# Layer 0 of a graph network: keys of two tiles of rows gathered with one weight load per block, and even and odd rounds of different order

## The chip, the cores and the metric

The kernel runs on one core of a Trainium2 chip. The metric is the device time of one execution in microseconds (us), as the median over several executions. The engines are TensorE (PE, with its weight loads as PEld), VectorE (DVE), ScalarE (ACT), GpSimd (POOL) and SyncE (SP); POOL and SP issue the DMAs.

## What is computed

There are 8192 nodes with 128 features, and an adjacency matrix of 8192 x 8192 int32 in which about one entry in 1024 is set (some 8 per row). Two graph attention layers follow one another; the change touches layer 0 alone.

```python
h = relu(layernorm(x))
e = (h @ Ws) @ (h @ Wt).T                      # Ws, Wt: 128 x 64
alpha = softmax(where(adj > 0, e, -9e15))      # over all 8192 nodes
x = x + alpha @ (h @ Wc)                       # layer 0
h = relu(layernorm(x))
# layer 1: another attention with leaky_relu scores, elu at the end, added to x
```

## The kernel before

**Tiles and selection.** The rows are worked on in 64 tiles of 128 rows. The nodes are held as 64 blocks (`NB`) of 128. For a tile the kernel doesn't score all 8192 nodes: from each block it picks up to 32 (`SLOT`) that some row of the tile has as a neighbour. For this DVE makes a 0/1 matrix `pick[:, b, block, slot]` (fp8, `make_pick`) out of the running count of marked nodes, which PE makes with one matmul against a triangle of ones (`prefix`) and DVE multiplies by the marks (`place`). A tile then has 64 x 32 = 2048 picked nodes.

**Gathering on PE.** The picks are matmul operands. `pick_keys(t, b, g)` has the keys `kp` of a block as weights (128 x 128) and 32 columns of `pick` as moving data, 16 blocks to a group, four groups g to a tile, and writes the PSUM bank `kg_ps`. `pick_values` and `pick_mask` have the pick as weights (32 columns of the array) and values or mask as moving data; each has four groups to a tile and one PSUM bank (`vg_ps`, `mg_ps`). ACT empties each bank after each group (`take_keys`, `take_values`, `take_mask`, 512 columns each), and the next group of the same kind waits for that: `wait(pe, k_evac, t * 4 + g)` and its likes.

**Scores and weighing.** `scores(t, b, q)` (q = 0 to 3) fills one of four PSUM banks from the gathered keys and mask; it waits for `k_evac` and `m_evac` of its group q and for the exponentials of the tile before. DVE takes the maximum of two banks at a time (`part_maximum`), spreads it (`spread_maximum`), PE transposes it (`turn_maximum`), DVE reduces it (`maximum`), ACT takes the exponentials of two banks at a time (`exps`), and PE weighs the values in four groups (`weigh`, 32 fp32 matmuls of 129 columns in all, of which the first group has one more). DVE divides and adds x (`denominator`, `finish`).

**Order.** Each engine runs the same sweep: round i works on tiles e = i-1, a = i-2, c = i-3 and d = i-4 at once, in an order written out by hand in `tile_step`. An engine does its instructions strictly in this order, waits included. Before, all rounds have one order; on PE it is: scores(c,3), values(c,2), mask(a,2), keys(a,1), values(c,3), mask(a,3), turn_maximum(c), keys(a,2), values(a,0), prefix(e), weigh(d,0 to 3), keys(a,3), scores(a,0), values(a,1), mask(e,0), scores(a,1), keys(e,0), mask(e,1), scores(a,2). Rounds 0 to 5 and 64 to 67 are written out, those between are a loop of two rounds. The first mask group of a tile waits for its `make_pick`.

**Adjacency.** POOL issues four DMAs per tile (`load_chunk`), each as soon as the mask group that read the same part of the buffer two tiles before is done.

Of the kernel before, what the change touches and what calls it, by code (L numbers as in the profile page):

```python
# [18 lines left out]
P = 128  # L19
# [28 lines left out]
def gnn_kernel(nc, x, xB, adj, adjB, Ws, Wt, Wc, W1, a1, out, x_mid, sel, sel_pick):  # L48
# [12 lines left out]
    with ExitStack() as ctx:  # L61
# [11 lines left out]
        def part(start, words, dt=F32):  # L73
# [5 lines left out]
            0, 8192, 16384, 20480, 28672, 32768, 34816, 36864, 40992, 43040, 44064, 45088, 46080)  # L79
# [14 lines left out]
        k_sel = part(K2, 1024, F16)  # L94
# [108 lines left out]
        kg_ps = ps[:, 4, :]  # L203
# [5 lines left out]
        mx_ps = ps[:, 7, 256:256 + P]  # L209
# [418 lines left out]
        def _(pe):  # L628
# [125 lines left out]
            def scores(t, b, q):  # L754

                pe.wait_ge(k_evac, t * 4 + (q + 1))
                pe.wait_ge(m_evac, t * 4 + (q + 1))
                wait(pe, p_done, t * 2 + (q // 2 - 1))
                settle()
                dst = s_ps[q]  # L760
                nc.tensor.matmul(dst, off_i, m_sel8[:, b, 4 * q:4 * q + 4, :].rearrange("p s n -> p (s n)"),  # L761
                                 start=True, stop=False, skip_group_check=True)
                for k in range(4):
                    at = (4 * q + k) * P
                    for n, rows in enumerate((cq_hi, cq_lo)):
                        last = nc.tensor.matmul(dst[:, k * P:(k + 1) * P], k_sel[:, at:at + P],  # L766
                                                rows[:, bass.ts(t, P)], start=False, stop=(n == 1),
                                                skip_group_check=True)
                last.then_inc(sc_done, 1)

            def turn_maximum(t):

                pe.wait_ge(mx_ready, t + 1)
                wait(pe, y_ready, t - 1)
                nc.tensor.transpose(mx_ps, mx_b[:, :], ident[:, :]).then_inc(mx_turned, 1)  # L775

            def weigh(t, b, g):

                pe.wait_ge(p_done, t * 2 + (g // 2 + 1))
                pe.wait_ge(v_evac, t * 4 + (g + 1))  # L780
                if g == 0:
                    wait(pe, y_ready, t)
                    pe.wait_ge(top_done, min(t + 2, TILES) if isinstance(t, int) else t + 2)
                    nc.tensor.matmul(pv_ps, ones_b[:, :], mean_rows[0], start=True, stop=False, skip_group_check=True)
                for k in range(4):
                    s = 4 * g + k
                    last = nc.tensor.matmul(pv_ps, p_T[:, s * P:(s + 1) * P], v_sel[:, b, s, :],  # L787
                                            start=False, stop=(s == SB - 1), skip_group_check=True)
                last.then_inc(pv_done, 1)

            def tile_step(i, b):
                e, a, c, d, cb = i - 1, i - 2, i - 3, i - 4, 1 - b
                if isinstance(i, int) and i == 2:
                    pe.wait_ge(mean_ready, 1)
                if isinstance(i, int) and i == 4:
                    pe.wait_ge(rows_ready, 1)
                if isinstance(i, int) and i == TILES + 2:
                    pe.wait_ge(m_evac, TILES * 4)
                    turn_weights(0, mg_ps)
                if isinstance(i, int) and i == TILES + 3:  # L800
                    score_vectors(0, mg_ps)
                if there(i, 3):
                    scores(c, cb, 3)
                    pick_values(c, cb, 2)
                if there(i, 2):
                    pick_mask(a, b, 2)
                    pick_keys(a, b, 1)
                if there(i, 3):
                    pick_values(c, cb, 3)
                if there(i, 2):  # L810
                    pick_mask(a, b, 3)
                if there(i, 3):
                    turn_maximum(c)
                if there(i, 2):
                    pick_keys(a, b, 2)
                    pick_values(a, b, 0)
                if within(i, EARLY + 1, TILES + 1):
                    prefix(e, pre_ps)
                if there(i, 4):
                    for g in range(4):  # L820
                        weigh(d, b, g)
                if there(i, 2):
                    pick_keys(a, b, 3)
                    scores(a, b, 0)
                    pick_values(a, b, 1)
                if there(i, 1):
                    pick_mask(e, cb, 0)
                if there(i, 2):
                    scores(a, b, 1)
                if there(i, 1):  # L830
                    pick_keys(e, cb, 0)
                    pick_mask(e, cb, 1)
                if there(i, 2):
                    scores(a, b, 2)
# [140 lines left out]
        def _(act):  # L975
# [132 lines left out]
            def take_keys(t, g):  # L1108

                act.wait_ge(kg_done, t * 4 + (g + 1))  # L1110
                nc.scalar.activation(k_sel[:, g * GW:(g + 1) * GW], kg_ps, ACT.Copy).then_inc(k_evac, 1)  # L1111
# [25 lines left out]
            def tile_step(i, b):  # L1137
                e, a, c, cb = i - 1, i - 2, i - 3, 1 - b
                if there(i, 3):
                    take_values(c, cb, 2)  # L1140
                if there(i, 2):
                    take_mask(a, b, 2)
                    take_keys(a, 1)
                if there(i, 3):
                    take_values(c, cb, 3)
                if there(i, 2):
                    take_mask(a, b, 3)
                    take_keys(a, 2)
                if there(i, 3):
                    exps(c, 0)  # L1150
                if there(i, 2):
                    take_values(a, b, 0)
                    take_keys(a, 3)
                if there(i, 3):
                    exps(c, 1)
                if there(i, 2):
                    take_values(a, b, 1)
                if there(i, 1):
                    take_mask(e, cb, 0)
                    take_keys(e, 0)  # L1160
                    take_mask(e, cb, 1)
# [140 lines left out]
        def _(dve):  # L1302
# [219 lines left out]
            def tile_step(i, b):  # L1522
# [3 lines left out]
                if there(i, 3):  # L1526
                    spread_maximum(c)
                if within(i, EARLY + 1, TILES + 1):
                    indicate(e, 1 - b, 1)
                if there(i, 3):  # L1530
# [17 lines left out]
                if there(i, 2):  # L1548
# [3 lines left out]
                if there(i, 2):  # L1552
                    part_maximum(a, 1)
# [421 lines left out]
```

## Time and the profile before

| | us |
|---|---|
| median of 3 runs | 1359.65 (1357.86 to 1359.94) |
| the profiled execution | 1364.51 |
| its span from first to last instruction | 1362.7 |
| around the span | 1.8 |
| mean granted TensorE clock | 0.979 |
| PE busy | 1270.7 (93%) |
| DVE busy | 1043.8 (77%) |
| ACT busy | 980.1 (72%) |

The first weighing of layer 0 starts at 108.6 us and the last at 903.5 us of the span; before it stands the preparation of the operands, behind it layer 1. Line 722 is the key matmul, 734 the values, 749 the mask, 761 and 766 the scores, 775 the transpose, 784 and 787 the weighing, 648 the prefix. ACT's lines are 1111 for keys, 1117 for values, 1126 for the mask and 1133 for the exponentials. DVE's are 1468 for `place`, 1477 for `make_pick` and 1486 for `part_maximum`.

In the timeline a row merges instructions of one kind that follow each other. Its duration for PE reaches to the end of the last matmul's results, while the next group starts earlier: the time that a group takes from PE is the distance to the start of the next row, where that did not wait.

### The profile page before, as it was taken

Reading aid. Unit: us, or ns where it says so; the run is one execution under the profiler, and the core shown is the slowest. Engines: PE = TensorE matmul, PEld = TensorE weight load, DVE = VectorE, ACT = ScalarE, POOL = GpSimd, SP = SyncE. Lnnn points to the kernel's source line nnn. Section 1 sums busy time; section 2 is a strip of 40 time slices with the busy share of each in tenths; the row PEclk is TensorE's granted clock in tenths of the full one; section 3 lists DMA queues with packets and bytes.
Section 4 is the critical chain, followed back from the end, with each engine's and each line's share of the span. In section 5 each row is a group of like instructions: output and inputs, shape, how many; then the busy total and the mean of one; then the engine's idle time right before and its main releaser. Section 6 shows DMA issues by size and latency. Waiting matters only on the chain.

```text
span 1362.7 us, 74732 instructions
## 1 busy us (share of the span) xinstructions
PE 1270.7 (93%) x31691; PEld 1125.0 (83%) x31691; DVE 1043.8 (77%) x2196; ACT 980.1 (72%) x2100; POOL 165.8 (12%) x331
## 2 busy tenths in 40 slices
PE   4868899999999999999999999988899999999996
PEld 3657788888888888888888888876899989999996
DVE  6846467767776766777777677657899989999997
ACT  4855466666666666666666666667898989999995
POOL 4210111111111111111111111012000000000000
PEclk9969899999999999999999999999899999999998
DMA  9773699999999999999999999610234334334332
GB/s 188 77 89 67 91 127 138 139 138 129 140 140 131 133 137 133 136 137 141 129 138 141 140 126 139 108 48 2 73 111 117 100 102 127 108 100 126 112 96 73
DMA packets 103503, 157.54 MB, mean 116 GB/s; under 512 B 11456, under 2 KB 36288, under 8 KB 102848
## 3 DMA queue, kind: packets, MB, share of 16 engines
q0 software_dynamic: 36864, 67.13, 52.4%
q1 hardware_dynamic: 66496, 88.37, 20.0%
q8 instruction: 107, 1.75, 0.5%
q14 instruction: 36, 0.29, 0.1%
HBM read 314.84 MB, written 41.94 MB: 262 GB/s over the span
## 4 chain that ended last, share of the span: by engine, by line
PE 76%; issue 9%; ACT 8%; DVE 4%; DMA 2%; POOL 1%; ACTq 0%; SPq 0%; DVEq 0%; POOLq 0%
PE ps L883 16%; PE ps L787 16%; PE ps L734 10%; PE ps L857 9%; PE ps L766 6%; PE ps L749 4%; PE ps L761 4%; PE ps L722 4%; ACT arena L1117 3%; ACT arena L1126 3%; PE ps L775 1%; DMA arena<-in_adjB 1%; PE ps L663 1%; PE ps L639 1%; PE ps L880 1%
## 5 line engine op out<-in xcount | busy, mean ns | idle before, releaser
L787 PE MATMUL ps<-arena 128*128 128x129 f32 x2048 | 246.6, 279 | 0.0
L883 PE MATMUL ps<-arena 128*128 128x129 f32 x2048 | 244.9, 278 | 0.7 <-issue 0.7
L1133 ACT ACTIVATE arena<-ps,neg_max 128x1024 f32<-128x1024 f32 x128 | 142.3, 1112 | 135.5 <-PE ps L787 135.5
L787 PEld LDWEIGHTS ps<-arena 128*128 128x128 f32 x2048 | 237.8, 194 | 0.0
L883 PEld LDWEIGHTS ps<-arena 128*128 128x128 f32 x2048 | 236.7, 194 | 0.9 <-issue 0.9
L1486 DVE TENSOR_REDUCE mx<-ps 128x1 f32<-128x1024 f32 x128 | 156.7, 1225 | 97.1 <-PE ps L766 92.7
L1117 ACT ACTIVATE arena<-ps 128x512 f32<-128x512 f32 x256 | 152.6, 596 | 100.9 <-PE ps L734 100.9
L589 POOL DMA_DIRECT2D arena<-in_adjB x256 | 136.6, 534 | 688.2 <-PE ps L749 672.6
L1691 DVE TENSOR_SCALAR arena<-arena 128x128 f32<-128x128 f32 x768 | 202.6, 341 | 15.0 <-issue 8.6
L1111 ACT ACTIVATE arena<-ps 128x512 f16<-128x512 f32 x256 | 153.6, 600 | 41.2 <-PE ps L722 38.6
L734 PE MATMUL ps<-arena 128*32 128x128 f16 x8192 | 164.7, 222 | 19.0 <-issue 9.3
L766 PEld LDWEIGHTS ps<-arena 128*128 128x128 f16 x2048 | 135.4, 98 | 31.0 <-issue 1.1
L1126 ACT ACTIVATE arena<-ps 128x512 fp8e4<-128x512 f32 x256 | 152.9, 597 | 10.9 <-PE ps L749 7.8
L857 PE MATMUL ps<-arena 128*32 128x132 f16 x8192 | 147.3, 226 | 14.2 <-ACT arena L1171 6.3
L1477 DVE TENSOR_TENSOR arena<-arena 128x2048 fp8e4<-128x2048 f16 x64 | 146.7, 2292 | 17.5 <-DVE arena L1468 17.3
L1171 ACT ACTIVATE arena<-ps 128x396 f32<-128x396 f32 (+1 forms) x384 | 144.6, 477 | 18.9 <-PE ps L857 18.9
L766 PE MATMUL ps<-arena 128*128 (+1 forms) x2048 | 157.7, 220 | 0.0
L1458 DVE TENSOR_REDUCE arena<-arena 128x32 f32<-128x1024 uint32 x128 | 154.9, 1210 | 1.6 <-DMA arena<-in_adjB 1.6
L734 PEld LDWEIGHTS ps<-arena 128*32 128x32 fp8e4 x8192 | 121.7, 97 | 40.1 <-issue 24.2
L857 PEld LDWEIGHTS ps<-arena 128*32 128x32 fp8e4 x8192 | 125.1, 98 | 32.4 <-ACT arena L1171 7.8
L1700 DVE SCALAR_TENSOR_TENSOR arena<-arena 128x1024 f32<-128x1024 fp8e4 x128 | 150.9, 1218 | 0.5 <-ACT arena L1191 0.5
L722 PE MATMUL ps<-arena 128*128 128x32 fp8e4 x4096 | 144.0, 177 | 0.6 <-issue 0.6
(164 smaller groups left out, 1321.8 us busy)
## 6 DMA issues: line engine op xcount, KB each, us to landing
arena<-in_adjB POOLq DMA_DIRECT2D x256, 256.0 KB, 8.1
sel_pick<-arena SPq DMA_DIRECT2D x64, 256.0 KB, 6.2
sel<-arena SPq DMA_DIRECT2D x64, 256.0 KB, 6.2
arena<-sel_pick SPq DMA_DIRECT2D x64, 256.0 KB, 3.5
arena<-sel SPq DMA_DIRECT2D x64, 256.0 KB, 2.7
arena<-in_xB SPq DMA_DIRECT2D x4, 1024.0 KB, 6.0
x_t<-in_x SPq DMA_DIRECT2D x64, 64.0 KB, 5.0
x_mid<-arena SPq DMA_DIRECT2D x64, 64.0 KB, 5.1
```

Of the source, the lines that this page charges most:

```text
L722: last = nc.tensor.matmul(kg_ps[:, k * SLOT:(k + 1) * SLOT], kp[:, g * SB + k, :], pick[:, b, g * SB + k, :], start=True, stop=True)
L734: last = nc.tensor.matmul(vg_ps[j * SLOT:(j + 1) * SLOT, s * D:(s + 1) * D], pick[:, b, k, :], c_vals[:, k, l * D:(l + 1) * D], start=(l = ...
L766: last = nc.tensor.matmul(dst[:, k * P:(k + 1) * P], k_sel[:, at:at + P], rows[:, bass.ts(t, P)], start=False, stop=(n == 1), skip_group_c ...
L787: last = nc.tensor.matmul(pv_ps, p_T[:, s * P:(s + 1) * P], v_sel[:, b, s, :], start=False, stop=(s == SB - 1), skip_group_check=True)
L857: last = nc.tensor.matmul(xg_ps[g % 3][j * SLOT:(j + 1) * SLOT, at:at + XW], pick[:, b, s * QB + j, :], wv[:, s * QB + j, l, :], start=(l ...
L883: last = nc.tensor.matmul(xv_ps[b], w_msk[:, b, s, :], x1_sel[:, b, s, 0:VW], start=False, stop=(s == SB - 1), skip_group_check=True)
L1111: nc.scalar.activation(k_sel[:, g * GW:(g + 1) * GW], kg_ps, ACT.Copy).then_inc(k_evac, 1)
L1117: nc.scalar.activation(v_sel[:, b, 4 * g:4 * g + 4, 0:D], vg_ps.rearrange("p (s v) -> p s v", v=D), ACT.Copy).then_inc(v_evac, 1)
L1126: nc.scalar.activation(m_sel8[:, b, 4 * q:4 * q + 4, :].rearrange("p s n -> p (s n)"), mg_ps, ACT.Copy, bias=-1.0, saturate=False).then_in ...
L1458: nc.vector.reduce_max(ind_raw[:, at], mask[:, at, :], AX_X).then_inc(ind_max, 1)
L1486: nc.vector.reduce_max(mx[:, h:h + 1], ps[:, 2 * h:2 * h + 2, :].rearrange("p b n -> p (b n)"), AX_X).then_inc(part_max, 1)
L1691: last = nc.vector.tensor_scalar(w_raw[b][:, k, :], own, x1_sel[:, b, k, D + 2:D + 3], x1_sel[:, b, k, D + 1:D + 2], ALU.mult, ALU.max)
```

## The change

`pick_keys` loses its tile argument b: a group has 8 blocks instead of 16, with 64 moving columns (32 of each of two tiles, an even one and the next) to each weight load, and there are eight groups g for two tiles instead of eight groups of 16 blocks. The group still fills one bank of 512 columns, and `take_keys` empties it into a `k_sel` of two halves. Scores q of either tile need groups 2q and 2q+1 of the pair. Both picks must be there before the first key group, and the first key group of an even tile is in the round in which the odd tile's pick is made.

The rounds differ. The even round has keys(a,0) and keys(a,1), the odd one keys(c,2) to keys(c,7) of the pair, where `c` is the same even tile one round later. The mask, values and weighing of a tile are spread over the rounds as the listing shows. On ACT and DVE the order follows. The transposed maximum moves from bank 7 to bank 6, which the mask groups and `prefix` use: `turn_maximum` waits for `m_evac` of the tile after, `prefix` for `top_done`, and `weigh` no longer waits for `top_done`.

```diff
-        k_sel = part(K2, 1024, F16)
+        k_sel = part(K2, 2048, F16).rearrange("p (u n) -> p u n", u=2)
-        kg_ps = ps[:, 4, :]
+        kg_ps = ps[:, 4, :].rearrange("p (u k s) -> p u k s", u=2, s=SLOT)
-        mx_ps = ps[:, 7, 256:256 + P]
+        mx_ps = ps[:, 6, 3 * P:4 * P]
...
                 if dst is pre_ps:
                     wait(pe, m_evac, t * 4)
+                    wait(pe, top_done, t - 1)
...
-            def pick_keys(t, b, g):
-
+            def pick_keys(t, g):
+
+                if g == 0:
+                    pe.wait_ge(pick_ready, t + 2)
                 wait(pe, k_evac, t * 4 + g)
                 settle()
-                for k in range(SB):
-                    last = nc.tensor.matmul(kg_ps[:, k * SLOT:(k + 1) * SLOT], kp[:, g * SB + k, :],
-                                            pick[:, b, g * SB + k, :], start=True, stop=True)
+                for k in range(8):
+                    last = nc.tensor.matmul(kg_ps[:, :, k, :], kp[:, g * 8 + k, :],
+                                            pick[:, :, g * 8 + k, :], start=True, stop=True)
...
             def scores(t, b, q):
 
-                pe.wait_ge(k_evac, t * 4 + (q + 1))
+                pe.wait_ge(k_evac, (t - b) * 4 + (2 * q + 2))
...
             def turn_maximum(t):
 
                 pe.wait_ge(mx_ready, t + 1)
-                wait(pe, y_ready, t - 1)
+                pe.wait_ge(m_evac, min(t + 2, TILES) * 4 if isinstance(t, int) else t * 4 + 8)
...
             def weigh(t, b, g):
...
-                    pe.wait_ge(top_done, min(t + 2, TILES) if isinstance(t, int) else t + 2)
...
+            def even_round(i, e, a, c, d):      # conditions on the first and last rounds left out
+                scores(c, 1, 3); pick_values(c, 1, 2); pick_mask(a, 0, 2); pick_values(c, 1, 3)
+                pick_mask(a, 0, 3); pick_values(a, 0, 0); weigh(d, 0, 0); turn_maximum(c)
+                weigh(d, 0, 1); weigh(d, 0, 2); prefix(e, pre_ps); weigh(d, 0, 3)
+                pick_values(a, 0, 1); pick_mask(e, 1, 0); pick_keys(a, 0); pick_mask(e, 1, 1)
+                pick_keys(a, 1); scores(a, 0, 0)
+
+            def odd_round(i, e, a, c, d):
+                pick_keys(c, 2); pick_mask(a, 1, 2); pick_keys(c, 3); scores(c, 0, 1)
+                pick_values(c, 0, 2); pick_keys(c, 4); pick_mask(a, 1, 3); pick_keys(c, 5)
+                scores(c, 0, 2); pick_values(c, 0, 3); pick_keys(c, 6); weigh(d, 1, 0)
+                pick_keys(c, 7); scores(c, 0, 3); pick_values(a, 1, 0); weigh(d, 1, 1)
+                weigh(d, 1, 2); turn_maximum(c); weigh(d, 1, 3); prefix(e, pre_ps)
+                pick_values(a, 1, 1); scores(a, 1, 0); scores(a, 1, 1); pick_mask(e, 0, 0)
+                scores(a, 1, 2); pick_mask(e, 0, 1)
...
+                # ACT, even round
+                take_values(c, 1, 2); take_mask(a, 0, 2); take_values(c, 1, 3); take_mask(a, 0, 3)
+                take_values(a, 0, 0); exps(c, 0); exps(c, 1); take_values(a, 0, 1)
+                take_mask(e, 1, 0); take_keys(a, 0); take_mask(e, 1, 1); take_keys(a, 1)
+                # ACT, odd round
+                take_keys(c, 2); take_mask(a, 1, 2); take_keys(c, 3); take_values(c, 0, 2)
+                take_keys(c, 4); take_mask(a, 1, 3); take_keys(c, 5); take_values(c, 0, 3)
+                take_keys(c, 6); take_keys(c, 7); take_values(a, 1, 0); exps(c, 0); exps(c, 1)
+                take_values(a, 1, 1); take_mask(e, 0, 0); take_mask(e, 0, 1)
...
             def make_pick(t, b):
+                wait(dve, kg_done, (t - b) * 4)
...
+                # DVE, in place of both part_maximum(a) at the end of every round
+                # even: part_maximum(c, 1) ahead of spread_maximum(c)
+                # odd:  part_maximum(c, 0), part_maximum(c, 1), spread_maximum(c) behind indicate(e);
+                #       part_maximum(a, 0) ahead of indicate(i)
```

## Rows read from the trace of the kernel before

**Rows 1.** The page, part 1: busy time, share of the span, instructions

```profile
PE 1270.7 (93%) x31691; PEld 1125.0 (83%) x31691; DVE 1043.8 (77%) x2196; ACT 980.1 (72%) x2100; POOL 165.8 (12%) x331
```

**Rows 2.** Windows: busy of PE, PEld, DVE, ACT, POOL; clock; DMA

```profile
155.00:165.00 10.00, 7.52 (x69) 7.20 (x69) 2.93 (x5) 1.88 (x3) 0.00 (x0) 0.66 0.60 101
...
300.00:600.00 300.00, 291.74 (x7834) 256.91 (x7832) 214.60 (x335) 202.28 (x336) 50.88 (x96) 1.00 1.04 136
```

**Rows 3.** Timeline of PE, one round of layer 0: start us, us, instructions

```profile
499.96 0.20 PE L648 MATMUL ps<-arena 128*128 128x64 f16 x1
...
500.15 3.79 PE L787 MATMUL ps<-arena 128*128 128x129 f32 x32
503.78 0.56 PE L722 MATMUL ps<-arena 128*128 128x32 fp8e4 x16
504.19 0.38 PE L761 MATMUL ps<-arena 128*128 128x512 fp8e4 x1
504.40 0.61 PE L766 MATMUL ps<-arena 128*128 x8
504.94 0.63 PE L734 MATMUL ps<-arena 128*32 128x128 f16 x32
505.39 0.40 PE L749 MATMUL ps<-arena 128*32 128x128 fp8e4 x16
505.72 0.39 PE L761 MATMUL ps<-arena 128*128 128x512 fp8e4 x1
505.95 0.61 PE L766 MATMUL ps<-arena 128*128 x8
506.40 0.56 PE L722 MATMUL ps<-arena 128*128 128x32 fp8e4 x16
507.10 0.41 PE L749 MATMUL ps<-arena 128*32 128x128 fp8e4 x16
...
511.19 0.33 PE L775 MATMUL ps<-ident,arena 128*128 128x128 f32 x1
511.36 0.56 PE L722 MATMUL ps<-arena 128*128 128x32 fp8e4 x16
...
512.42 0.20 PE L648 MATMUL ps<-arena 128*128 128x64 f16 x1
```

**Rows 4.** Timeline of ACT in the same round

```profile
504.37 0.60 ACT L1111 ACTIVATE arena<-ps 128x512 f16<-128x512 f32 x1 [0.58 <-PE ps L722]
504.87 1.11 ACT L1133 ACTIVATE arena<-ps,neg_max 128x1024 f32<-128x1024 f32 x1
505.87 0.60 ACT L1117 ACTIVATE arena<-ps 128x512 f32<-128x512 f32 x1
506.34 0.61 ACT L1126 ACTIVATE arena<-ps 128x512 fp8e4<-128x512 f32 x1
```

**Rows 5.** Chain of waits in the same round: start us, us, what

```profile
509.62 0.61 ACT arena L1117
510.23 0.14 issue
```

**Rows 6.** Timeline of DVE in the same round

```profile
500.21 0.23 DVE L1468 TENSOR_TENSOR arena<-ps,arena 128x64 f16<-128x64 f32 x1 [0.39 <-PE ps L648]
500.72 2.29 DVE L1477 TENSOR_TENSOR arena<-arena 128x2048 fp8e4<-128x2048 f16 x1 [0.29 <-DVE arena L1468]
...
506.60 1.22 DVE L1486 TENSOR_REDUCE mx<-ps 128x1 f32<-128x1024 f32 x1 [1.21 <-PE ps L766]
```

**Rows 7.** DMA of 400 to 700 us: queue with its engine share; issues to landing

```profile
q0 software_dynamic: 13719, 24.98, 88.9%
...
arena<-in_adjB POOLq DMA_DIRECT2D x96, 256.0 KB, 8.0
```

**Rows 8.** Timeline of PE behind its longest idle time in the sweep

```profile
157.48 0.59 PE L734 MATMUL ps<-arena 128*32 128x128 f16 x13 [4.56 <-issue]
...
158.13 6.16 PE L787 MATMUL ps<-arena 128*128 128x129 f32 x32
```

More of the change, by code:

```diff
@@ L830, in tile_step @@
                 if there(i, 1):
-                    pick_keys(e, cb, 0)
-                    pick_mask(e, cb, 1)
+                    pick_mask(e, 1, 1)
                 if there(i, 2):
-                    scores(a, b, 2)
+                    pick_keys(a, 1)
+                    scores(a, 0, 0)
+            def odd_round(i, e, a, c, d):
+                if there(i, 3):
+                    pick_keys(c, 2)
+                if there(i, 2):
+                    pick_mask(a, 1, 2)
+                if there(i, 3):
+                    pick_keys(c, 3)
+                    scores(c, 0, 1)
+                    pick_values(c, 0, 2)
+                    pick_keys(c, 4)
+                if there(i, 2):
+                    pick_mask(a, 1, 3)
+                if there(i, 3):
+                    pick_keys(c, 5)
+                    scores(c, 0, 2)
+                    pick_values(c, 0, 3)
+                    pick_keys(c, 6)
+                if there(i, 4):
+                    weigh(d, 1, 0)
+                if there(i, 3):
+                    pick_keys(c, 7)
+                    scores(c, 0, 3)
+                if there(i, 2):
+                    pick_values(a, 1, 0)
+                if there(i, 4):
+                    weigh(d, 1, 1)
+                    weigh(d, 1, 2)
+                if there(i, 3):
+                    turn_maximum(c)
+                if there(i, 4):
+                    weigh(d, 1, 3)
+                if within(i, EARLY + 1, TILES + 1):
+                    prefix(e, pre_ps)
+                if there(i, 2):
+                    pick_values(a, 1, 1)
+                    scores(a, 1, 0)
+                    scores(a, 1, 1)
+                if there(i, 1):
+                    pick_mask(e, 0, 0)
+                if there(i, 2):
+                    scores(a, 1, 2)
+                if there(i, 1):
+                    pick_mask(e, 0, 1)
@@ L1148, in tile_step @@
-                    take_keys(a, 2)
+                    take_mask(a, 1, 3)
+                if there(i, 3):
+                    take_keys(c, 5)
+                    take_values(c, 0, 3)
+                    take_keys(c, 6)
+                    take_keys(c, 7)
+                if there(i, 2):
+                    take_values(a, 1, 0)
                 if there(i, 3):
                     exps(c, 0)
-                if there(i, 2):
-                    take_values(a, b, 0)
-                    take_keys(a, 3)
@@ L1154, in tile_step @@
-                if there(i, 3):
                     exps(c, 1)
                 if there(i, 2):
-                    take_values(a, b, 1)
+                    take_values(a, 1, 1)
                 if there(i, 1):
-                    take_mask(e, cb, 0)
-                    take_keys(e, 0)
-                    take_mask(e, cb, 1)
+                    take_mask(e, 0, 0)
+                    take_mask(e, 0, 1)
             first_preparation()
@@ L1525, in tile_step @@
                     return
-                if there(i, 3):
+                if there(i, 3) and b == 0:
+                    part_maximum(c, 1)
                     spread_maximum(c)
@@ L1529, in tile_step @@
                     indicate(e, 1 - b, 1)
+                if there(i, 3) and b == 1:
+                    part_maximum(c, 0)
+                    part_maximum(c, 1)
+                    spread_maximum(c)
                 if there(i, 3):
@@ L1547, in tile_step @@
                     finish(d, b)
-                if there(i, 2):
+                if there(i, 2) and b == 1:
                     part_maximum(a, 0)
```

82 lines of the change are left out of this document (54 added, 28 removed).

## The prediction

> **What bounds the kernel now.** I read the page first: PE is busy for 93% of the span [rows 1]. The windows then show that the steady part of layer 0 has PE at 292 of 300 us with the full clock, DVE at 72% and ACT at 67% [rows 2]. A busy PE row includes the drain of results, so I took the timeline and looked at starts only. One round lasts 12.46 us (from prefix to prefix), and by the starts its PE work is [rows 3]: weighing 3.63 and its extra matmul 0.12; prefix 0.14; transpose 0.17; four key groups of 0.41; four score groups of 0.66 (0.21 for the wide one, 0.45 for eight of 128 columns); four value groups of 0.46; four mask groups of 0.34. That is 11.54 us. The missing 0.92 us are waits of PE for ACT. The reader is to see one of them: keys start at 506.40, would be through at 506.81, and the mask group starts only at 507.10, because ACT took the mask bank late [rows 3, 4]. So the bound is PE's work in one fixed order, with little waiting, and what matters is whether a new order keeps it so.
>
> **The price of a round trip.** A bank that one PE group fills and the next step needs emptied costs: 0.18 us from the end of the group's issue to ACT's start (keys end at 504.19, ACT starts at 504.37), 0.60 us for ACT, 0.15 us until PE starts again [rows 3 to 5]. That is 0.93 us, less whatever PE has in between. ACT takes one such bank each 0.49 us when they queue up, and 1.01 us for an exponential [rows 4]. From the start of prefix to the end of `make_pick` it is 3.05 us, and 3.20 us until PE can use it [rows 3, 6].
>
> **What is removed.** For two tiles there were 128 key matmuls of 32 columns at 25.6 ns (0.41 us for 16), 3.28 us. There are now 64 of 64 columns. The trace shows none of these; 25.6 ns (32 columns) and 56 ns (128 columns, 0.45 us for 8) are its bounds [rows 3]. I take 30 ns, near the closer row, so 0.24 us for a group of 8 and 1.92 us for the pair (bounds 1.64 and 3.6). Work falls by 1.36 us for a pair of rounds, from 23.1 to 21.7 us.
>
> By the back-to-back issue gap in the Trainium skill, page "TensorE: Matmul & The Clock Gate", matmuls of 1 to 64 columns all cost about 60 cycles, some 25 ns; the row of 32 columns agrees with 25.6 ns, and 64 columns would then be 1.6 us for the pair. The sum would be about 10 us lower over the kernel, so this rule settles nothing here.
>
> **What is added: waits.** ACT has as many banks to empty as before (eight key banks for a pair), and PE's order now has places where a group directly follows what it needs. I walk through a pair of rounds, PE in its new order, ACT and DVE in theirs, with the prices above; each stall is PE standing.
>
> Even round. Values(c,3) stand behind values(c,2) and one mask group: 0.93 less 0.34 gives 0.6; before, a key group stood between as well. The same for values(a,0) behind values(c,3): 0.6. Prefix now stands behind three of the four weighings. After it come its own 0.14, one weighing 0.91 and values 0.46, 1.51 us in all, and then mask(e,0) wants the pick that takes 3.20 us: 1.7 stall. Before, the whole weighing and more lay there, 5.4 us (prefix at 499.96, the mask at 505.39), so it was free. Mask(e,1) behind mask(e,0) and one short key group: 0.93 less 0.24, 0.7. Keys(a,1): ACT takes mask(e,0) first and keys(a,0) second: 0.15. Scores(a,0) directly behind keys(a,1), which ACT takes behind mask(e,1): 1.05. With rounding that is 4.8.
>
> Odd round. Keys(c,3) behind keys(c,2) and one mask group: 0.6. Scores(c,1) directly behind keys(c,3): 0.95. Keys(c,5): ACT takes values(c,2) ahead of keys(c,4): 0.86. Scores(c,2) directly behind keys(c,5): 0.95. Keys(c,7), with one weighing as cover: 0.17. Scores(c,3) directly behind keys(c,7): 0.95. Then DVE's maximum, which now begins only here: part_maximum 1.23 [rows 6], the transpose in its place in PE's order behind two weighings, reduction, exponential; scores(a,0) want that exponential out of their banks: 0.57. Mask(e,0): prefix plus 3.20 again, against 0.14 of its own, values 0.46 and two scores 1.32, and 0.57 of stall already stood: 0.7. Mask(e,1) behind mask(e,0) and scores(a,2): 0.93 less 0.66, 0.3. Together 6.05.
>
> The pair: 21.7 of work and 10.9 of stalls, 32.6 us, against 24.92 before. The same walk through the order before gives 24.56 instead of 24.92, so I add its miss of 0.36. The four scores have three semaphore waits ahead of them, of which the late one is now the first; I put some 0.05 us on each. That makes 33.2, or **8.3 us more for each pair**.
>
> Other edits. The new waits of `turn_maximum` (mask banks empty), of `prefix` (`top_done`) and of `make_pick` (`kg_done`) end before their places in the walk; no cost. In the even round `turn_maximum` comes 1.9 us behind the spread maximum, and `top_done` is 1.5 us ahead of prefix; without that cover each would stall PE and what is queued there. The DMAs: q0 uses 88.9% of the engines' time, and a chunk lands 8.0 us after issue [rows 7]. A pair that is 33 us long leaves them more time, though four chunks are now asked for within some 5 us (masks at the end of the odd and the start of the even round). At 2.8 us of queue time each (0.889 x 12.46 / 4) the last lands some 15 us after the first is issued, and DVE wants it after about the same time, in a stretch in which it then waits for scores anyway: no cost. SP's stores keep their places and are not waited for closely.
>
> **The sum.** Key groups belong to rounds 2 to 65, 32 pairs. In the first, PE also stands for reasons that the change leaves (4.56 us in one place [rows 8]) and that hide some of the stalls; I count 31. 31 x 8.3 = 257 us. The profiled execution takes 1364.5 (span 1362.7 and 1.8 around it) and would take 1622; the median of the runs is 4.9 lower, so 1617 us.
>
> **Rivals.**
> - *The waits are hidden, as most are now*, and only the work counts: 32 x 1.36 = 43 us less, 1316 us. For it: four key waits before the change are nearly free. Against: before, each scores group had at least the whole weighing or one other group between it and its keys; now nothing stands there, and no other instruction of PE can step in. It decides only if a round trip costs less than about 0.93 x 1.36 / 10.9, 0.12 us, where the rows show 0.93. The DMA would not stop it: 88.9% of 12.46 is 11.1 us a tile, under 11.8. Chance 3%.
> - *Half the stalls*: ACT or the semaphores are quicker where nothing queues, or I have misplaced cover such as the pick. Stalls of 5.5 instead of 10.9 give +2.9 a pair, 1450 us. Chance 7% for anything from no change to 1560. No change itself needs stalls of about 3.2 us a pair: 1%.
> - *The clock falls.* PE stands for a third of the time. After idling 4.56 us it ran the next weighing in 6.16 us instead of 3.79, at a granted clock of 0.66 over that stretch, the lower level being 1.2 GHz [rows 2, 3, 8]. My longest stall is 1.7 us. If one weighing per pair ran so, 2.4 x 31 = 73 us more, 1690 us; more work at that level gives 1750. Chance 9%.
> - *The 64-column matmul costs as one of 128*: 3.6 instead of 1.92, partly hidden under the waits for ACT, about +0.8 a pair, 1642 us. Chance 8%.
> - *The forecast*, 1565 to 1700: 72% on top of these.
>
> Against the gain speaks also a rule of the Trainium skill, page "Trainium Kernel Development and Optimization", best practices: faster TensorE work does not speed up emptying PSUM. The trace agrees in that ACT's bank takes 0.60 us whatever PE saves, and the change leaves ACT's count of banks as it is. By that rule alone the time would not fall, which is between the rivals above.
>
> **Range and chances.** Low end: stalls an eighth cheaper (1.4) and keys at 25.6 ns (0.3) give 6.6 a pair, 205 us, 1565 us. High end: the dear keys (25 us more) together with a clock that falls in most pairs for part of a weighing (58 us), 1700 us. The forecast and the dear keys lie within 1565 to 1700, some 80%; the hidden or half stalls lie below, a clock that falls often above. A change under 0.2% is about what a measurement of this kernel can't tell from none. Faster 4%, same 1%, slower 95%.
>
> **What the profile would show.** Rounds of about 14.2 and 19 us in turn. PE's busy time in the steady stretch falls from 97% to 65 to 80% (the rows contain drains), with the clock still at 1.00. In the timeline of PE, gaps of about 0.9 us ahead of each L761 that follows a key group, and 1.7 us ahead of the first mask group of the even round. Four key banks' `take_keys` rows with PE waiting for each. Key matmuls halved to 4096, starting 25 to 36 ns apart. The forecast is wrong if gaps at these places are under 0.5 us, if the pick is ready before PE wants it, or if the clock in the sweep is under 0.95.

## The result and the profile after

The changed kernel takes 1763.64 us (median of 3 runs, 1757.06 to 1763.87) against 1359.65, a ratio of 1.297 (95% interval 1.293 to 1.301): 404 us slower. I had forecast 1617 us, 257 us slower, with 1565 to 1700 as the range. The direction was right, but the time lies above the range: some 147 of the 404 us were missing from the forecast.

The page of the changed kernel, part 1 and two lines of digits of part 2 (against [rows 1]):

```profile
PE 1419.0 (81%) x29643; PEld 1192.8 (68%) x29643; DVE 1038.2 (59%) x2196; ACT 1009.4 (57%) x2100; POOL 164.9 (9%) x331
...
PE   5767777777777777777777777777788999999997
...
PEclk9888878877887887788788778878798999999999
```

PE has 2048 matmuls fewer and is busy for longer, 1419 us instead of 1271. That can't be waiting, since waiting is not busy. The second line of digits says what it is: the granted clock is at 0.7 to 0.8 all through layer 0. The windows of the changed kernel put it at (against [rows 2]):

```profile
300.00:600.00 300.00, 230.32 (x4620) 186.94 (x4621) 137.55 (x215) 138.93 (x219) 33.24 (x64) 0.80 0.72 90
```

Its timeline of PE, from the prefix of an even round on (against [rows 3]; in brackets the idle time before a row and what ended it):

```profile
615.47 0.19 PE L649 MATMUL ps<-arena 128*128 128x64 f16 x1
615.50 1.14 PE L789 MATMUL ps<-arena 128*128 128x129 f32 x8
616.57 0.63 PE L737 MATMUL ps<-arena 128*32 128x128 f16 x32
618.75 0.41 PE L752 MATMUL ps<-arena 128*32 128x128 fp8e4 x16 [1.55 <-DVE arena L1556]
619.09 0.41 PE L725 MATMUL ps<-arena 128*128 128x64 fp8e4 x8
620.11 0.41 PE L752 MATMUL ps<-arena 128*32 128x128 fp8e4 x16 [0.61 <-ACT arena L1178]
620.60 0.58 PE L725 MATMUL ps<-arena 128*128 128x64 fp8e4 x8
622.05 0.59 PE L764 MATMUL ps<-arena 128*128 128x512 fp8e4 x1 [0.87 <-ACT arena L1162]
622.43 1.06 PE L769 MATMUL ps<-arena 128*128 x8
...
626.06 0.59 PE L764 MATMUL ps<-arena 128*128 128x512 fp8e4 x1 [0.78 <-ACT arena L1162]
626.44 1.06 PE L769 MATMUL ps<-arena 128*128 x8
627.43 1.04 PE L737 MATMUL ps<-arena 128*32 128x128 f16 x32
...
636.29 0.38 PE L764 MATMUL ps<-arena 128*128 128x512 fp8e4 x1 [0.78 <-ACT arena L1162]
636.50 0.61 PE L769 MATMUL ps<-arena 128*128 x8
637.04 0.63 PE L737 MATMUL ps<-arena 128*32 128x128 f16 x32
...
645.98 0.38 PE L764 MATMUL ps<-arena 128*128 128x512 fp8e4 x1 [0.47 <-issue]
```

Two things stand in these rows. First, the stalls are where the walk had them. The mask waits for the pick (L1556) until 618.75, 3.28 us after prefix. The second mask waits for ACT, and every scores group (L764) behind its keys (L725) waits for the keys' evacuation (L1162). Second, from about 621 to 634 us everything lasts nearly twice as long: a scores group takes 1.37 us (626.06 to 627.43) instead of 0.75 (636.29 to 637.04), one matmul row of eight 1.06 instead of 0.61. The windows of 2.5 us over the same stretch show it:

```profile
615.00:617.50 2.50, 2.20 (x47) 1.89 (x45) 1.41 (x2) 1.65 (x2) 0.00 (x0) 1.00 1.07 107
617.50:620.00 2.50, 0.75 (x24) 0.55 (x24) 2.10 (x6) 1.48 (x4) 0.42 (x1) 1.00 0.99 125
620.00:622.50 2.50, 1.44 (x26) 0.99 (x27) 2.27 (x3) 1.62 (x3) 0.63 (x2) 0.63 0.87 199
622.50:625.00 2.50, 2.27 (x40) 1.94 (x39) 0.00 (x0) 0.99 (x2) 0.11 (x1) 0.50 1.04 118
...
632.50:635.00 2.50, 2.50 (x50) 2.24 (x49) 0.00 (x0) 1.08 (x2) 0.00 (x0) 0.64 0.77 77
635.00:637.50 2.50, 1.72 (x52) 1.39 (x50) 0.35 (x1) 0.60 (x1) 0.00 (x0) 1.00 0.00 0
```

A clock of 0.50 is the lower level, 1.2 GHz. PE was busy for 0.75 us of the window from 617.50 to 620.00, still at 1.00; the clock fell within the next window. No single idle time there was above 1.55 us. The clock came back while PE was weighing. This happens in every pair of rounds. A pair takes 37.6 to 37.9 us (scores at 608.18 and at 645.98) with a granted clock of 0.82, and in every fourth pair, where the slow stretch lasts longer, 40.3 at 0.75; before it was 25.04.

### The profile page after: what moved, and what is told of

The parts are those of the page before. It is cut to its first block, busy times and chain, and to the rows that moved or that the text cites. A ratio compares the mean times of both kernels' runs of the same rounds, so it can differ in the third digit from the quotient of the medians.

```text
span 1762.2 us, 70952 instructions
## 1 busy us (share of the span) xinstructions
PE 1419.0 (81%) x29643; PEld 1192.8 (68%) x29643; DVE 1038.2 (59%) x2196; ACT 1009.4 (57%) x2100; POOL 164.9 (9%) x331
## 4 chain that ended last, share of the span: by engine, by line
PE 62%; ACT 13%; DVE 11%; issue 11%; DMA 1%; ACTq 0%; POOL 0%; DVEq 0%; SPq 0%; POOLq 0%
PE ps L934 13%; PE ps L789 12%; PE ps L737 9%; DVE arena L1556 8%; PE ps L908 7%; PE ps L769 6%; ACT arena L1162 6%; PE ps L764 4%; PE ps L725 4%; ACT arena L1178 3%; PE ps L752 3%; ACT arena L1169 2%; PE ps L664 1%; PE ps L931 1%; PE ps L639 1%
## 5 line engine op out<-in xcount | busy, mean ns | idle before, releaser
L789 PE MATMUL ps<-arena 128*128 128x129 f32 x2048 | 276.6, 288 | 0.0
L789 PEld LDWEIGHTS ps<-arena 128*128 128x128 f32 x2048 | 259.5, 201 | 4.3 <-issue 1.4
L934 PE MATMUL ps<-arena 128*128 128x129 f32 x2048 | 244.9, 278 | 1.2 <-issue 1.2
L934 PEld LDWEIGHTS ps<-arena 128*128 128x128 f32 x2048 | 236.7, 194 | 1.3 <-issue 1.3
L737 PE MATMUL ps<-arena 128*32 128x128 f16 x8192 | 191.1, 245 | 42.5 <-ACT arena L1169 40.0
L764 PE MATMUL ps<-arena 128*128 128x512 fp8e4 x256 | 117.7, 460 | 133.5 <-ACT arena L1162 103.6
L1162 ACT ACTIVATE arena<-ps 128x512 f16<-128x512 f32 x256 | 152.3, 595 | 106.9 <-PE ps L725 103.0
L769 PE MATMUL ps<-arena 128*128 (+1 forms) x2048 | 202.9, 256 | 0.0
L769 PEld LDWEIGHTS ps<-arena 128*128 128x128 f16 x2048 | 169.8, 116 | 44.2 <-issue 19.5
L752 PE MATMUL ps<-arena 128*32 128x128 fp8e4 x4096 | 118.9, 244 | 94.0 <-DVE arena L1556 63.8
L737 PEld LDWEIGHTS ps<-arena 128*32 128x32 fp8e4 x8192 | 141.4, 108 | 77.1 <-issue 63.0
L1556 DVE TENSOR_TENSOR arena<-arena 128x2048 fp8e4<-128x2048 f16 x64 | 146.7, 2292 | 22.2 <-DVE arena L1546 11.8
L908 PE MATMUL ps<-arena 128*32 128x132 f16 x8192 | 147.4, 226 | 14.2 <-ACT arena L1249 6.3
L725 PE MATMUL ps<-arena 128*128 128x64 fp8e4 x2048 | 140.0, 227 | 19.7 <-ACT arena L1162 17.6
```

What stands on the lines that cost most here:

```text
L725: last = nc.tensor.matmul(kg_ps[:, :, k, :], kp[:, g * 8 + k, :], pick[:, :, g * 8 + k, :], start=True, stop=True)
L737: last = nc.tensor.matmul(vg_ps[j * SLOT:(j + 1) * SLOT, s * D:(s + 1) * D], pick[:, b, k, :], c_vals[:, k, l * D:(l + 1) * D], start=(l = ...
L908: last = nc.tensor.matmul(xg_ps[g % 3][j * SLOT:(j + 1) * SLOT, at:at + XW], pick[:, b, s * QB + j, :], wv[:, s * QB + j, l, :], start=(l ...
L934: last = nc.tensor.matmul(xv_ps[b], w_msk[:, b, s, :], x1_sel[:, b, s, 0:VW], start=False, stop=(s == SB - 1), skip_group_check=True)
L1162: nc.scalar.activation(k_sel[:, :, g * 2 * P:(g + 1) * 2 * P], kg_ps.rearrange("p u k s -> p u (k s)"), ACT.Copy).then_inc(k_evac, 1)
L1556: nc.vector.tensor_tensor(pick[:, b, :, :], posx.unsqueeze(2).to_broadcast(wide), slots[:, :].unsqueeze(1).to_broadcast(wide), ALU.is_equa ...
```

## The theories

A: the loss is waits of the new order (a round trip through ACT wherever something stands directly behind what it needs, and the late pick), and these waits pull the clock down in each pair, which costs the other third. B: the 146 us that the forecast lacks are further waits, and the clock follows them without being a cost of its own. C: the wide key matmuls or the buffers themselves are dear, in any order. Each kernel ran in 3 rounds against the kernel before on the same chip, the last two in 5. The edits below are shown without their conditions on the first and last rounds (`if there(...)`) and without keyword arguments that all unused matmuls have.

## Is the clock a cost of its own?

The first kernel gives PE something to do in the stall ahead of the mask:

```diff
+            def fill(n):
+                for k in range(n):
+                    nc.tensor.matmul(spare_ps, kp[:, k, :], cq_hi[:, 0:P], ...)    # spare_ps = ps[:, 4, 0:P]
...
                     pick_values(a, 0, 1)
+                    fill(28)
                     pick_mask(e, 1, 0)
```

> The changed kernel with 28 matmuls of 128 columns more in each even round, between values(a,1) and mask(e,0), where PE stands for some 1.6 us; their result is not used. Theory A (the 146 us that the prediction missed are the clock, which falls in each pair of rounds after the wait for the pick): 28 x 56 ns = 1.57 us fit into the stall and cost nothing, the granted clock stays at 1.00 in the sweep, a pair takes 33.2 us instead of 37.8, and the time is 1763 - 31 x 4.6, about 1620 us. Rival B (the missing time is further waits of the new order, and the clock only follows them): 1763 us or somewhat more. Rival C (it is the whole share of idle time that pulls the clock down, wherever it lies): the clock still falls, at a later place, 1700 to 1760 us.

Measured: 1658.34 us (1656.44 to 1663.18), ratio 1.219 (1.215 to 1.223). More work made the kernel 105 us faster. The mask starts after the fillers (L813) with no idle time left, and the next stalls and scores groups run at the full clock:

```profile
610.04 1.74 PE L813 MATMUL ps<-arena 128*128 128x128 f16 x28
611.71 0.41 PE L753 MATMUL ps<-arena 128*32 128x128 fp8e4 x16
...
616.83 0.39 PE L726 MATMUL ps<-arena 128*128 128x64 fp8e4 x8 [0.44 <-ACT arena L1170]
618.00 0.38 PE L765 MATMUL ps<-arena 128*128 128x512 fp8e4 x1 [0.78 <-ACT arena L1170]
618.22 0.61 PE L770 MATMUL ps<-arena 128*128 x8
618.76 0.63 PE L738 MATMUL ps<-arena 128*32 128x128 f16 x32
```

The clock over 300 to 600 us was 0.96, not 1.00. Most pairs take 34.4 us at 1.00, but in a few it still fell (35.9 us at 0.91, 39.6 at 0.78). The next kernel fills the four waits of the even tiles' scores as well:

```diff
             def scores(t, b, q):
-                pe.wait_ge(k_evac, (t - b) * 4 + (2 * q + 2))
+                dst = s_ps[q]
                 pe.wait_ge(m_evac, t * 4 + (q + 1))
                 wait(pe, p_done, t * 2 + (q // 2 - 1))
+                if b == 0:
+                    settle()
+                    for k in range(13):
+                        nc.tensor.matmul(dst[:, 0:P], kp[:, k, :], cq_hi[:, 0:P], ...)
+                pe.wait_ge(k_evac, (t - b) * 4 + (2 * q + 2))
```

> The changed kernel with unused matmuls in five stalls: 28 ahead of mask(e,0) in the even round, and 13 ahead of each scores group of the even tiles, while it waits for its keys (into the bank that the scores then overwrite). Theory A (without any fall of the clock a pair takes 34.4 us, and the rest of the loss is round trips): granted clock 1.00 in the sweep, about 1645 us, 10 to 15 below the kernel with one filled stall, where the clock still fell in some pairs. Rival B (the filling delays the work behind it): above 1660 us.

Measured: 1648.77 us (1647.30 to 1651.19), ratio 1.212 (1.210 to 1.214). From the fourth pair on all but the last take 34.28 us, and the windows show the full clock:

```profile
300.00:600.00 300.00, 256.25 (x5859) 214.22 (x5860) 155.41 (x246) 153.19 (x245) 36.57 (x69) 1.00 0.77 99
```

So of the 404 us some 115 are the clock (1763.6 less 1648.8) and 287 (1648.8 less this run's 1361.6 before) are the order at the full clock. The added matmuls do not lengthen the pair: where only the first stall is filled, the pairs at full clock take the same 34.4 us. Theory B has fallen. The last kernel of this group has the fillers in the scores' waits alone and leaves the 1.6 us ahead of the mask empty.

> The changed kernel with unused matmuls only ahead of the scores groups of the even tiles (13 each, while they wait for their keys), and the stall ahead of mask(e,0) left empty. Theory A (what pulls the clock down is the idle time from the wait for the pick to the first scores; filling only what comes later keeps it from falling again and shortens the slow stretch): clock in the sweep between 0.85 and 0.97, 1660 to 1710 us. Rival B (only the pick stall matters, so filling elsewhere gives nothing): clock 0.80 in the sweep and 1760 us. Rival C (the share of idle time alone matters; 52 fillers here are more than the 28 that brought 1658): 1650 to 1660 us.

Measured: 1653.46 us (1652.49 to 1655.52), ratio 1.218 (1.216 to 1.220), granted clock 1.00 and 0.99 in the two windows. My A was wrong here, and the time is that of C: it is not the one longest stall. With that stall left open and later ones filled, the clock stays up in nearly all pairs. C's reason, the share of idle time alone, is not shown by this. Over 300 to 600 us PE was idle for 23% in the changed kernel at a clock of 0.80, and two kernels of the next sections have 24% at 0.94 and 27% at 0.88. What in the pattern of the waits decides stays open.

## What are the waits?

Prefix earlier in the even round, so that three weighings cover the making of the pick:

```diff
+                turn_maximum(c)
                 weigh(d, 0, 0)
-                turn_maximum(c)
+                prefix(e, pre_ps)
                 weigh(d, 0, 1)
                 weigh(d, 0, 2)
-                prefix(e, pre_ps)
                 weigh(d, 0, 3)
```

> The changed kernel with turn_maximum(c) ahead of weigh(d,0) and prefix(e) right behind weigh(d,0) in the even round, so that three weighings cover the making of the pick. Theory A: the stall of 1.6 us ahead of mask(e,0) goes, 0.7 us of it come back ahead of mask(e,1), where ACT still has the second exponential ahead of the mask; 1.05 x 31 = 33 us, and if the shorter stall also keeps the clock up, 142 us more, so about 1590 us; with the clock still falling about 1730 us. Rival B (prefix is not what is late): 1760 us.

Measured: 1650.45 us (1647.01 to 1651.85), ratio 1.213 (1.209 to 1.217), 113 us less than the changed kernel; the clock over 300 to 600 us is 0.94. That lies between my two figures, because the clock still falls in nearly every pair, only for a shorter time: most pairs take 34.2 us at 0.95, three of them 37.1 at 0.82, and three have 1.00 throughout and take 33.2. Those three are 1.06 us shorter than the 34.28 of the filled kernel, where I had expected 1.05. The stall did what the walk said. It went from the first mask group, and the wait ahead of the second grew from 0.61 to 1.22:

```profile
602.40 0.40 PE L752 MATMUL ps<-arena 128*32 128x128 fp8e4 x16
602.73 0.41 PE L725 MATMUL ps<-arena 128*128 128x64 fp8e4 x8
604.35 0.41 PE L752 MATMUL ps<-arena 128*32 128x128 fp8e4 x16 [1.22 <-ACT arena L1176]
```

Value groups between keys and scores at three places of the odd round:

```diff
                 pick_keys(c, 3)
-                scores(c, 0, 1)
                 pick_values(c, 0, 2)
+                scores(c, 0, 1)
...
                 # the same for pick_values(c, 0, 3) and scores(c, 0, 2),
                 # and for pick_values(a, 1, 0) and scores(c, 0, 3)
```

> The changed kernel with a value group between keys and scores at three places of the odd round: keys(c,3), values(c,2), scores(c,1), and likewise values(c,3) ahead of scores(c,2) and values(a,0) ahead of scores(c,3). Theory A (a scores group directly behind its keys pays a round trip of 0.95 us): each of the three stalls falls to 0.49 us and that ahead of keys(c,5) by 0.25, 1.7 us a pair, 53 us, so about 1710 us with the clock as in the changed kernel. Rival B (these stalls are no loss since something else, such as ACT, is the bound there): within 10 us of 1763.

Measured: 1611.18 us (1606.79 to 1613.47), ratio 1.184 (1.180 to 1.188), 152 us less. The stalls ahead of the scores fell from 0.78 to 0.22 or nothing. The one pair of the sweep with a clock of 1.00 throughout takes 31.88 us, 2.40 less than the 34.28 of the filled kernel. That is 74 us over 31 pairs, where I had expected 1.7 us and 53; the rest of the 152 is the clock (0.92 instead of 0.80), which I had left out of this expectation.

Both edits together:

> The changed kernel with both earlier edits: prefix ahead of three weighings in the even round, and a value group between keys and scores at three places of the odd round. Theory A (the stalls are of separate places, so their savings add; the clock recovers further because less idle time is left): the walk gives 3.1 us less a pair than the changed kernel at full clock, so a pair near 31.3 us and 1550 us, up to 1580 if the clock still falls in some pairs. Rival B (one of the two places takes over what the other frees): no better than the better of the two, 1611 us.

Measured: 1535.72 us (1532.71 to 1537.10), ratio 1.129 (1.127 to 1.131). Better than either, so the places are separate: at full clock the two edits save 1.06 and 2.40 us a pair, and together 3.51. From the sixth pair on all but the last are alike, 30.77 us, where I had expected 31.3. Here is the window:

```profile
300.00:600.00 300.00, 234.81 (x5791) 197.88 (x5790) 172.93 (x270) 173.12 (x276) 41.29 (x79) 1.00 0.85 112
```

PE is busy for 78% of it, hardly more than the 77% of the changed kernel, but at the full clock. The row has 5791 matmuls in the 300 us against 4620: a busy share does not tell how fast the engine works.

## The same waits in the kernel before

If the order is the cause, it must hurt without the wide matmuls. First the late prefix alone, in the kernel before:

```diff
                 pick_values(a, b, 0)
+                for g in range(3): weigh(d, b, g)
                 prefix(e, pre_ps)
-                for g in range(4): weigh(d, b, g)
+                weigh(d, b, 3)
```

> The kernel before with one edit: prefix behind three of the four weighings, as in the changed kernel's even round. Theory A (the pick takes 3.20 us from prefix, and what is not covered is a stall): covered are prefix 0.14, a weighing 0.91, keys 0.41, scores 0.66 and values 0.46, so 0.6 us of stall ahead of mask(e,0) and, of it, 0.4 us a round in the period; 62 rounds, 25 us, 1385 us, clock unchanged. Rival B (a late pick costs the clock even when the stall is short): 1440 us or more. Rival C (hidden): 1360 us.

Measured: 1382.85 us (1382.14 to 1383.77), ratio 1.016 (1.015 to 1.018), 21 us more, with the clock at 1.00. The mask now waits for the pick, 3.19 us behind the prefix that starts at 615.11:

```profile
615.11 0.19 PE L648 MATMUL ps<-arena 128*128 128x64 f16 x1
...
617.27 0.63 PE L734 MATMUL ps<-arena 128*32 128x128 f16 x32
618.30 0.41 PE L749 MATMUL ps<-arena 128*32 128x128 fp8e4 x16 [0.40 <-DVE arena L1479]
```

Then the adjacency alone, with the key matmuls of before:

```diff
+                pick_keys(c, cb, 3)
                 scores(c, cb, 3)
...
-                pick_keys(a, b, 1); pick_keys(a, b, 2); pick_keys(a, b, 3); pick_keys(e, cb, 0)
...
                 # and pick_keys(a, b, q) directly ahead of scores(a, b, q) for q = 0, 1, 2
```

> The kernel before, with its own key matmuls (16 blocks, 32 columns, a weight load for each tile) but each key group directly ahead of the scores that need it: keys(c,3) scores(c,3), keys(a,0) scores(a,0), keys(a,1) scores(a,1), keys(a,2) scores(a,2), on ACT accordingly. Theory A (the loss of the change is the adjacency of keys and scores and not the wide matmuls): four round trips of 0.93 to 1.5 us a round; the walk gives 35.7 us for a pair of rounds against 24.9, so about 1695 us at full clock, and up to 100 more if the clock falls. Rival B (the order is harmless where the keys are narrow): under 1450 us.

Measured: 1781.47 us (1777.43 to 1782.96), ratio 1.308 (1.305 to 1.311). The old key matmuls in an order of this kind are as slow as the changed kernel, and they too lose the clock (0.88 over 300 to 600 us). The likeness of the two times has no meaning of its own, for here eight scores groups of a pair stand directly behind their keys, and in the changed kernel four. How much of the 420 us is the clock was not separated. Its timeline:

```profile
607.11 0.56 PE L722 MATMUL ps<-arena 128*128 128x32 fp8e4 x16
609.23 0.38 PE L761 MATMUL ps<-arena 128*128 128x512 fp8e4 x1 [1.55 <-ACT arena L1111]
...
610.79 0.57 PE L722 MATMUL ps<-arena 128*128 128x32 fp8e4 x16
612.48 0.38 PE L761 MATMUL ps<-arena 128*128 128x512 fp8e4 x1 [1.13 <-ACT arena L1111]
```

## What are the wide key matmuls worth?

In the changed kernel's own order, with each weight loaded twice and 32 columns each time:

```diff
                 for k in range(8):
-                    last = nc.tensor.matmul(kg_ps[:, :, k, :], kp[:, g * 8 + k, :], pick[:, :, g * 8 + k, :], ...)
+                    for u in range(2):
+                        last = nc.tensor.matmul(kg_ps[:, u, k, :], kp[:, g * 8 + k, :], pick[:, u, g * 8 + k, :], ...)
```

> The changed kernel's order with the key matmuls as before: each block's keys loaded twice, with 32 moving columns each time. Theory A (in this order the shared weight load is mostly hidden under waits for ACT): by the walk at full clock +0.75 us a pair, 23 us, so 1785 us, a few us more for the stretch at the lower clock. Rival B (the saved weight loads count in full): 1.36 x 31 = 42 us at full clock, 1805 us or more. Rival C (64 columns cost as much as twice 32): 1763 us.

Measured: 1749.06 us (1747.38 to 1755.61), ratio 1.285 (1.281 to 1.289) against 1.297 (1.293 to 1.301): the narrow matmuls are faster, by about 15 us. None of my three had that sign. The granted clock of the whole run is 0.871 instead of 0.856, and the pairs of the two traces say where the difference lies. At a granted clock of 0.82 a pair takes 37.8 to 38.1 us with narrow matmuls and 37.6 to 37.9 with wide ones. But with narrow ones every third pair has 0.86 and takes 36.84 us, and with wide ones every fourth has 0.75 and takes 40.3. So the clock is low for less time, which outweighs longer first pairs (42.5 and 41.4 us against 39.9 and 37.9 for the second and third); that the added matmuls do this because they stand in waits is argued, not shown. What the wide ones are worth in this order at the full clock was not measured.

So I looked for an order that keeps PE busy, with the changed kernel's buffers, waits and wide matmuls. Its rounds on PE:

```
even: V(c,0) M(a,0) S(c,2) M(a,1) V(c,1) S(c,3) M(a,2) V(c,2) M(a,3) W(d,0) T(c) V(c,3) P(e)
      W(d,1) W(d,2) V(a,0) K(a,0) V(a,1) K(a,1) M(e,0) K(a,2) W(d,3) K(a,3)
odd:  V(c,2) K(c,4) W(d,0) K(c,5) M(a,1) S(c,0) K(c,6) S(c,1) K(c,7) M(a,2) S(c,2) S(c,3)
      M(a,3) V(c,3) W(d,1) T(c) W(d,2) P(e) W(d,3) S(a,0) S(a,1)
```

(K keys, V values, M mask, S scores, W weighing, T transpose, P prefix; ACT and DVE follow.) 

> The changed kernel's buffers, waits and wide key matmuls in another order of the two rounds, in which no scores group stands directly behind its keys, a weighing or a value group lies between most groups of one bank, and prefix has three weighings, keys and values behind it. Theory A (the loss is the order's waits): the walk leaves 0.3 us of stalls a pair and 26.8 us in all, so 27.0 with its usual miss, clock 1.00, 1363 + 31 x 1.95 = 1423 us; it stays above the kernel before because changing between full weights and 32-column weights some 30 times costs about 0.09 us each. Rival B (the arrangement has a further cost that no order removes, such as the keys of both tiles falling together): 1500 us or more. Rival C (the changes between weight kinds cost nothing when nothing waits): 1340 to 1370 us.

Measured: 1415.85 us (1414.03 to 1418.36), ratio 1.043 (1.042 to 1.044). A pair takes 26.89 us, at the full clock:

```profile
300.00:600.00 300.00, 272.50 (x6619) 226.75 (x6617) 201.30 (x315) 197.84 (x314) 47.70 (x92) 1.00 1.00 127
```

With buffers, waits and wide matmuls as in the changed kernel, another order alone takes away 348 of the 404 us, so theory C has fallen too. And the same with narrow matmuls:

> The same order with narrow key matmuls (each block's keys loaded twice, 32 columns each time). Theory A (where PE hardly waits the shared weight load counts nearly in full): 1.3 us a pair more than with the wide ones, 40 us, 1463 us. Rival B (a matmul of 64 columns costs nearly as much as two of 32): under 10 us more.

Measured: 1471.43 us (1466.26 to 1473.31), ratio 1.083 (1.081 to 1.085), 56 us more than with the wide ones. A pair takes 28.1 us, or 29.1 where the clock falls, which it does in some pairs (0.98 to 0.99 in the windows). So the shared weight load is worth 1.2 us a pair, 38 us, once PE has work between its waits; the rest of the 56 us is the lower clock in seven later pairs, and the first pairs (the third takes 38.2 us at 0.91 against 30.2 at 1.00). The price of a wide matmul is read from a key row followed directly by a weighing in the first of these two kernels, 0.23 us for eight, 29 ns each:

```profile
607.27 0.39 PE L725 MATMUL ps<-arena 128*128 128x64 fp8e4 x8 [0.44 <-ACT arena L1164]
607.50 1.14 PE L789 MATMUL ps<-arena 128*128 128x129 f32 x8
608.48 0.40 PE L725 MATMUL ps<-arena 128*128 128x64 fp8e4 x8
608.80 0.63 PE L737 MATMUL ps<-arena 128*32 128x128 f16 x32
609.65 0.39 PE L725 MATMUL ps<-arena 128*128 128x64 fp8e4 x8 [0.22 <-ACT arena L1164]
```

Followed by a value group, the same eight take 0.32 us (608.48 to 608.80).

That kernel still loses 57 us to the one before. Its rows show what is left. First, waits: of a pair PE is idle for 2.5 us against 0.7 before (27.5 and 8.3 of 300 us in the windows), which is by size the whole 1.84 us that the pair is longer. Four waits of 0.22 to 0.44 us are for ACT; key groups of 0.24 us are too short to cover 0.6 us on ACT. One of 0.56 is the first key group waiting for the pick of the odd tile, and one of 0.28 is `prefix` waiting for `top_done`; both waits are new with the change. My expectation had only 0.3 us of stalls in its 26.8, so its total came out with a wrong split between waits and the rest. Second, changes between full weights and 32-column weights. Values followed by a mask group take 0.46 us (609.00 to 609.46 in the changed kernel's trace), and followed by a weighing 0.56 (637.04 to 637.60). How the 57 us divide between the two was not tried by a run, and no version beat the kernel before.

## Why the prediction was wrong

- **Wrong: the clock.** This is the step that failed. The sum left the clock at 1.00, and the rival "the clock falls" stood at 9%, with 73 us for one weighing in each pair and 1750 us in all for more work at the lower level. Its argument was "my longest stall is 1.7 us" against a row of 4.56 us idle. The clock fell in every pair, to 0.80 over the sweep, and cost about 115 us, as the filled kernels show (1649 to 1658 against 1764). The measured time lies within 1% of that second figure, for which the prediction had no working, and the prediction's own sign of being wrong, a clock in the sweep under 0.95, is the one that came true. The longest stall was the wrong thing to look at: leaving it open and filling four shorter ones brought the clock back too (1653 us). The walk already had PE idle for a third of the time, 8.1 of the 10.9 us between the late pick and scores(c,3), and the rival made no use of it. The Trainium skill, page "TensorE: Matmul & The Clock Gate", section "A second HAM failure mode: psum-queue depth-cycling", tells of short idles of TensorE between groups of matmuls that cycle through PSUM, with which the clock swings between its two levels. The trace agrees (0.50 behind stalls of 1.55, 0.61 and 0.87 us); I had weighed only single long gaps.
- **Right: the round trip.** 0.93 us from the end of keys to scores. Measured in the filled kernel: keys at 616.83 and scores at 618.00, so 1.17 with 0.24 of its own work.
- **Right: the late pick.** 3.20 us from prefix; 3.28 measured in the changed kernel and 3.19 in the kernel before with that edit.
- **Mis-sized: the pair.** 33.2 us forecast, 34.28 measured at the full clock. And the pair before takes 25.04, not 24.92: I had doubled one round of 12.46 us, but rounds of 12.46 and 12.58 alternate. So the loss at full clock is 9.2 us a pair instead of 8.3, 29 us over the kernel. Two things account for most of the 1.1 us. PE stands for 0.47 us at the start of the even round, idle time put down to issue (645.98), where the loop of two rounds begins again. And four value groups of a pair are followed at once by full weights and take 0.56 us; I had taken 0.46 everywhere.
- **Right: the price of a wide matmul**, 30 ns forecast, 29 measured (in the last order). Whether the 1.36 us a pair that I booked as saved came in, in the changed kernel's order, is not shown: the narrow kernel differs from it in the clock as well. In the last order 1.2 us of it did.
- **Right: no cost** for the DMAs and for the new waits of `turn_maximum`, `prefix` and `make_pick`: the idle times of PE in a pair name none of them. In the last order `prefix` did wait for `top_done`, 0.28 us.
- The pattern at full clock would have been 1649 us, within my range. Its rounds, counted from scores(c,3) to the first keys of the odd round, in the filled kernel are 14.4 and 19.9 us (forecast 14.2 and 19); in the changed kernel they are 15.1 and 22.7.
- A slip without effect on the sum: the key matmuls were halved from 4096 to 2048, not to 4096.

## What to carry to other kernels

Fewer instructions on the bound engine pay only if its order still puts work between each group and what waits for it: write down the round trip (here 0.93 us through ACT, 3.2 us for the pick) and look in the new order for every pair that stands closer. When a walk shows TensorE idle for a large part of a stretch, even in waits of 0.2 to 1.6 us, give a fall to the lower clock level a price and a real chance, and test it by filling a wait with unused matmuls. Here the walk said a third, and the clock was 0.80.

## What was not expected of the hardware

- Unused matmuls made a kernel 105 us faster (28 in each pair of rounds), since the granted clock stayed at 1.00 in most pairs, 0.96 over 300 to 600 us instead of 0.80.
- The clock fell without any idle time above 1.55 us. It also fell in the kernel before with another order and narrow matmuls (0.88), and did not in the steady part of the kernel with both edits, where PE is idle for 22% of the sweep, nearly as much as in the changed kernel (23%).
- PE is idle for 0.44 to 0.49 us, put down to issue, at one place of each pair, where the loop of two rounds begins again and PE had just waited for ACT. In the kernel before, where PE is not waiting there, every other round is 0.12 us longer (12.58 and 12.46 us). That both are the loop's own cost is inferred from their place.
